# VectorE's rope products ahead of the low parts of keys and queries in every period of a two-attention transformer block

## What is computed

```python
def _rope(x, sin, cos):
    xe, xo = x[..., ::2], x[..., 1::2]
    re = xe * c - xo * s
    ro = xe * s + xo * c

def _attn(xq, ctx, wq, wkv, wo, bo):
    q = _heads(xq @ wq)
    k, v = jnp.split(ctx @ wkv, 2, axis=-1)
    ...
    q, k = _rope(q, sq, cq), _rope(k, sk, ck)
    sim = jnp.einsum('bhnd,bhmd->bhnm', q, k) * DH ** (-0.5)
    a = jax.nn.softmax(sim, axis=-1)
    o = jnp.einsum('bhnm,bhmd->bhnd', a, v)
    return o @ wo + bo
```

## Time and profile before

| what | value |
|---|---|
| median of 3 runs | 1086.78 us (1084.18 to 1087.85) |
| the profiled execution, its own time | 1084.96 us |
| its span from the first to the last instruction | 1082.1 us |
| granted TensorE clock, mean | 0.998 |
| PE busy | 1069.5 us, 99% of the span |
| DVE busy | 848.2 us, 78% |
| POOL busy | 778.9 us, 72% |
| ACT busy | 645.5 us, 60% |
| PE's share of the chain that ended last | 94% |

### The profile page before, as it was taken

The page is one execution under the profiler, slowest core; times in us unless marked ns, Lnnn a source line. Parts: engine busy times, 40 slices in busy tenths (PEclk is TensorE's granted clock), DMA queues, the critical chain, the costliest instruction groups (busy, mean ns, idle before and its releaser), DMA issues.

```text
span 1082.1 us, 18353 instructions
## 1 busy us (share of the span) xinstructions
PE 1069.5 (99%) x6904; PEld 762.6 (70%) x6904; DVE 848.2 (78%) x1002; ACT 645.5 (60%) x928; POOL 778.9 (72%) x503
## 2 busy tenths in 40 slices
PE   8899999999999999999999999999999999999999
PEld 7667766776667666776667766666777666667998
DVE  5788777878787787787888888888888887887555
ACT  6575576666666555576766555665555546686521
POOL 2687777788887887689989966887678767765210
PEclk9999999999999999999999999999999999999999
DMA  5321122211222112211121112121121111300001
GB/s 173 97 69 40 31 55 57 63 42 33 55 69 43 27 41 52 57 36 34 41 69 35 40 36 69 41 50 40 40 56 43 40 40 40 100 20 1 20 21 39
DMA packets 61111, 52.85 MB, mean 49 GB/s; under 512 B 23520, under 2 KB 44000, under 8 KB 60768
## 3 DMA queue, kind: packets, MB, share of 16 engines
q1 hardware_dynamic: 59248, 50.10, 19.4%
q10 hardware_dynamic: 1776, 1.59, 0.5%
HBM read 15.75 MB, written 2.10 MB: 16 GB/s over the span
## 4 chain that ended last, share of the span: by engine, by line
PE 94%; DVE 2%; ACT 2%; issue 1%; DMA 1%; ACTq 0%; SPq 0%
PE ps L1052 19%; PE ps L838 10%; PE ps L840 9%; PE ps L839 9%; PE ps L991 6%; PE ps L1025 6%; PE ps L1039 6%; PE ps L913 6%; PE ps L997 5%; PE ps L993 5%; PE ps L995 5%; PE ps L1149 4%; PE ps L854 1%; PE ps L884 1%; PE ps L926 1%
## 5 line engine op out<-in xcount | busy, mean ns | idle before, releaser
L666 ACT ACTIVATE probs<-ps 128x1024 f32<-128x1024 f32 x256 | 262.6, 1027 | 196.7 <-PE ps L997 176.6
L1247 DVE TENSOR_REDUCE neg_max<-ps 128x2 f32<-128x1024 f32 x256 | 300.5, 1223 | 46.2 <-PE ps L1025 46.2
L517 POOL TENSOR_TENSOR acc<-acc,probs 128x1024 f32<-128x1024 f32 x126 | 300.5, 2385 | 18.1
L1052 PE MATMUL ps<-probs,v 128*64 128x512 f32 x1024 | 230.7, 592 | 0.0
L512 POOL TENSOR_TENSOR acc<-probs 128x1024 f32<-128x1024 f32 x64 | 152.4, 2381 | 48.7 <-ACT probs L666 48.7
L1052 PEld LDWEIGHTS ps<-probs,v 128*64 128x64 f32 x1024 | 73.9, 137 | 145.4 <-issue 145.4
L526 POOL TENSOR_TENSOR eo<-tmp 128x512 f32<-128x512 f32 x63 | 87.1, 1382 | 118.7 <-DVE tmp L1274 117.8
L1274 DVE TENSOR_TENSOR tmp<-ps,rope 128x1024 f32<-128x1024 f32 x126 | 148.4, 1213 | 17.0 <-PE ps L884 12.5
L1025 PE MATMUL ps<-hi 64*128 64x512 f32 x512 | 110.2, 413 | 2.8 <-DVE x L1291 1.1
L991 PE MATMUL ps<-max_rows,pick 64*128 64x512 f32 x512 | 109.8, 414 | 1.7 <-DMA max_rows<-neg_max 1.5
L838 PE MATMUL ps<-xn_hi,w_hi 128*128 128x512 f32 x256 | 106.7, 417 | 1.5 <-DVE xn_lo L363 1.5
(11 more groups left out here) (134 smaller groups left out, 2188.7 us busy)
## 6 DMA issues: line engine op xcount, KB each, us to landing
lo<-eo SPq DMA_DIRECT2D x126, 256.0 KB, 3.2
w_raw<-pack_dram SPq DMA_DIRECT2D x16, 192.0 KB, 3.4
x<-x_dram SPq DMA_DIRECT2D x4, 512.0 KB, 7.8
w_raw<-pack_dram SPq DMA_DIRECT2D x8, 256.0 KB, 3.8
max_rows<-neg_max SPq DMA_DIRECT2D x128, 2.0 KB, 2.1
w_raw<-w_dram SPq DMA_DIRECT2D x2, 1024.0 KB, 5.3
out<-x SPq DMA_DIRECT2D x7, 256.0 KB, 2.3
ctx_in<-ctx_dram SPq DMA_DIRECT2D x4, 384.0 KB, 4.0
```

Of the source, the lines that this page charges most:

```text
L517: pool.tensor_tensor(acc[:, g % 2, :, :], acc[:, g % 2, :, :], probs[:, i, :, :], ALU.add).then_inc(added, 1)
L666: act.activation(probs[:, i, :, :], score_ps(i), ACT.Exp, scale=SCALE).then_inc(exped, 1)
L1052: mm = pe.matmul(av_ps(g)[DH * h:DH * h + DH, :], v[:, u % 2, kt, c:c + DH], probs[:, kt, h, :], start=(kt == 0), stop=(kt == TT - 1))
L1247: dve.tensor_reduce(neg_max[:, g % 2, :, i], peak_ps(i), AX.X, ALU.max, negate=True).then_inc(maxed, 1)
```

## The change

DVE's `period(p)` had `low_qk(p + 2)` ahead of the two `rotate` of job p + 4, but for the periods in `stats_in`, where it stood behind them. Now it stands behind them in all.

```diff
                 if p == PAIRS - 2:
                     low_ffw(dve, 0)
-                if is_pair(p + 2) and p not in stats_in:
-                    low_qk(p + 2)
                 if is_job(p + 4):
                     rotate(p + 4, 0)
                     rotate(p + 4, 1)
-                if is_pair(p + 2) and p in stats_in:
+                if is_pair(p + 2):
                     low_qk(p + 2)
                 if p in out_in:
                     add_out(out_in[p], 0)
                     add_out(out_in[p], 1)
```

## The result

The changed kernel takes 1095.61 us (median of 5 runs, 1094.18 to 1096.13), the kernel before 1084.18 us (5 runs, 1082.35 to 1087.85). The ratio is 1.0094 with a 95% interval from 1.0077 to 1.011. The forecast was 1097 us, 1090 to 1105, on a kernel before of 1086.78; the change costs 11.4 us by the medians (8.3 to 11.9 by the interval) where 10.7 had been worked out. The profiled execution took 1094.18 us with a span of 1092.4 us, 10.3 us more than the span before.

What follows compares the result with a forecast made beforehand. PE, busy 1069.5 of 1082.1 us, was taken as the bound, so time could only be lost by making it wait. 11.2 - 1.0 + 2.0 - 0.5 - 1.0 = +10.7 us gave 1097 us, range 1090 to 1105.

Steps and rivals of the forecast that it cites:

- The even swapped periods, 1.12 us each: Even periods 36 to 54: later maxima make PE's step 2 0.92 us late, restart adds 0.2; 11.2 us for ten.
- the 2.2 to 2.4 us that I had named as a sign: Expected distance between PE's `peak` steps 1 and 2 in odd periods 37 to 55, instead of 1.28 us.
- POOL loses the race: In period 42 POOL starts 0.17 us behind the moved subtraction, which takes 1.21 us; 2.06 us as the other end.
- Rival C: In even periods 36 to 54 POOL's `eo` starts first, delaying subtraction and maxima: ten times 1.1 us, 1108 us; chance 8%.
- The odd swapped periods, 0.1 us gained each: Odd periods 37 to 55: products come first, additions to x end earlier; 0.1 us gained each, -1.0 us.
- The five periods with a rest of keys and an output, 0.41 us each: Periods 28, 30, 34, 56, 58: PE's step 0 0.21 us late for an addition to x, restart 0.2; +2.0 us.
- My own list of signs: Profile signs; prediction wrong if step 2 stays despite later maxima, other period pairs grow, or the moved subtraction takes 2 us.
- Periods 2 and 32: The subtraction no longer meets a busy POOL: -1.0 us in period 2, -0.5 us in period 32.
- "All other periods: nothing.": Remaining self-attention periods: the subtraction moves into the wait for PE's output, costing PE nothing.
- "no cost": POOL ends `eo` 0.9 us later, but PE wants the sum of its next additions only after its scores.
- A: PE's `peak` step 2 isn't held up, only small gains remain: 2.5 us, 1084.3 us on the median; chance 8%.
- B: Cheaper shared reading by DVE and POOL shortens the five longest even periods 1 us each: 1079 us; chance 4%.

## Why the prediction was right

*The even swapped periods, 1.12 us each.* Measured 1.10. The two halves of it were a little off in opposite directions: PE's step 2 came 0.81 us late, not 0.92, since DVE had 0.32 us in hand instead of 0.21 (I had put 0.15 us between the end of a maximum and PE's start; it is 0.05, while 0.15 holds behind an addition to x), and the restart took 0.29 us instead of 0.2 (steps 2 and 3 are 1.40 us apart instead of 1.15). So steps 1 and 2 are 2.09 us apart, below the 2.2 to 2.4 us that I had named as a sign. Moving these ten alone gives a loss as large as the whole; putting them back takes nearly all of it away.

*POOL loses the race.* Right: POOL's start was 0.16 us behind in period 42, and all the subtractions there took 1.22 us. Rival C stays unmeasured in its own size: where POOL was put first the subtraction read 2.27 us, as C had it, but that kernel also waits 1.4 us more in each period and lost clock, so its 40 us are not C's 11. The rule of the Trainium skill ("SBUF — State Buffer", section "SBUF: two separate sides"), that whoever starts first has the shared ports for the whole instruction, agrees with the cases met here: 0.03 us ahead left the subtraction at 1.22 us, 0.07 us behind made it 2.27. Wherever POOL was clearly first, the whole subtraction ended 1.07 to 1.09 us behind POOL's instruction. Once, in the run with the even periods put back, the trace has POOL 0.01 us ahead and DVE still took its 1.22 us; that is as fine as the times are given.

*The odd swapped periods, 0.1 us gained each.* Measured 0.8 us in all instead of 1.0, in the nine even periods behind them.

*The five periods with a rest of keys and an output, 0.41 us each.* The mechanism was right, as the run with the subtraction behind the additions shows, but the term was too small: 0.52 to 0.58 us, 2.8 us in all instead of 2.0, again by the restart (PE's step 0 was 0.27 to 0.29 us late in four of them and 0.38 in period 35, instead of 0.21, and the rest came on top). My own list of signs called the prediction wrong if pairs of periods outside the swapped ones grow, which these five do by the prediction's own term; that sign was badly put.

*Periods 2 and 32.* -1.07 and -0.34 us, for -1.0 and -0.5. The first depends on the execution that one compares with: three traces in which period 2 keeps its old order have the same 1.0 us less in period 3, behind a longer period 1. How many executions of the kernel before have the long period 3, no run here tells.

*"All other periods: nothing."* This failed in both directions. Periods 7, 11, 15 and 19 gained 0.75 us in all, since behind periods 6, 10, 14 and 18 too the second addition to x had been a tenth or so late for PE's step 1; period 36 gained 0.5 us, since the products of period 35 had been late for step 0. And period 17 lost 0.39 us. That last was the sentence "no cost" on POOL's 0.9 us: POOL, held up in period 15, came late to its bias (L536) in period 16, held the subtraction for 0.7 us there, and PE's step 0 waited: it came 0.05 us late, and step 1 another 0.2 us. The changed kernel, end of period 16:

```profile
295.25 2.40 POOL L536 TENSOR_TENSOR x<-x,bias_rows 128x1024 f32<-128x1024 f32 x1
...
296.82 1.91 DVE L1265 TENSOR_TENSOR lo<-lo,hi 128x1024 fp32r<-128x1024 f32 x1
```

In all, these terms that I had put at nothing come to -0.9 us, and the five periods above to 0.8 us more than forecast. That the two meet, so that the traces differ by 10.4 us where 10.7 was forecast, is luck.

*Rivals A and B.* PE's slack was about as small as rows 4 had it, 0.32 us, so A fell. Of B it is true that the shared reading got cheaper, by 21 us of DVE, though POOL's L526 took 46 us more. The kernel gets from it only the gains of single periods named above (the largest in 3, 33 and 36), not the 5 us of B.

## What to carry to other kernels

A wait of an engine that is not the bottleneck is a place where work costs nothing; before moving an instruction out of it, ask what stands behind the new place and how long the bottleneck's next wait on it can be put off. Here 1.22 us of work left an idle time of 1.25 us and went to where 0.32 us were to spare, ten times. The same move paid in some periods, as where the subtraction had met a busy POOL in its old place, so decide such an order by kinds of period, not for all at once: that gave 0.36% over the kernel before.

## What the runs showed of the hardware that I had not expected

A stall costs more than its own length. Where a step of TensorE was held up by 0.27 to 0.82 us, another 0.2 to 0.3 us went before the old distance between steps was back, and no more for the long ones than for the short: the next step came 1.39 us later behind 0.27 us (half a subtraction) and 1.40 us behind 0.82 us, instead of 1.15. A wait of 3.2 us cost its length and then a clock of 0.50 for 3.4 us, so that 2.56 us more of stall made the period 3.9 to 4.2 us longer. Two engines that read SBUF at once didn't share the loss: 0.03 us ahead or 0.07 us behind decided which one of them took its plain time and which one nearly twice that.

What stays open: the kernel with the ten periods put back was 1.3 us slower than the kernel before, although the sum over its periods has it only 0.2 us longer from period 0 to 63; most of the rest lies ahead of period 0. In the first 65 us of every kept trace the granted clock is at its lower level for 3.4 us (as in the kernel before) to 17.1 us, not always at the same place. The mean clock of the execution doesn't account for the 1.3 us: among executions of equal mean clock (0.992 to 0.993, 0.994 to 0.995, 0.997, 0.998) this kernel's are still slower by 0.3 to 1.8 us. Whether the move makes this difference, no run here shows.
